# Operations of a fused attention and mixture-of-experts kernel moved within the engines' orders: bias columns, norm seeds, tanh, parts of the first units, mask rows

## The reference, cut to what matters

```
x = x + xattn(ctx, layernorm(x), mask, mask, W_src, b_src, W_tgt, b_tgt, W_out, b_out)   # x: 8 x 512 x 256
x = x + ffn(layernorm(x), gate_w, w_gate, w_up, w_down, sw_gate, sw_up, sw_down)

xattn: k, v = split((ctx @ W_src.T + b_src) * mask);  q = (x @ W_tgt.T + b_tgt) * mask    # 8 heads of 32
       scores = where(mask == 0, -inf, q k / sqrt(32));  update = softmax(scores) v
       out = concat([x, update]) @ W_out.T + b_out
ffn:   scores = sigmoid(l2norm(x) @ l2norm(gate_w).T);  the 8 largest of 16, divided by their sum = combine
       out = sum over 16 experts of combine_e * (silu(x Wg_e) * (x Wu_e)) Wd_e  +  a shared expert without combine
```

## Time and profile before

| | us |
|---|---|
| median of 3 runs (lowest, highest) | 1065.43 (1065.13, 1066.44) |
| profiled execution, span from its first to its last instruction | 1056.2 |
| what lies around the span (median less span) | 9.2 |
| PE busy, share of the span | 1012.5, 96% |
| DVE, ACT, POOL busy | 647.5, 465.9, 389.0 |
| mean granted clock of PE, of full speed | 0.992 |

### The profile page before, as it was taken

One profiled execution on the slowest core, in us unless ns is written; L12 is line 12 of the kernel. 1 busy time (PEld: TensorE's weight loads), 2 busy tenths in 40 slices (PEclk: granted clock), 3 DMA queues, 4 the chain that ended last, 5 costly groups with the idle time before them and its releaser, 6 DMA issues.

```text
span 1056.2 us, 14941 instructions
## 1 busy us (share of the span) xinstructions
PE 1012.5 (96%) x5198; PEld 773.3 (73%) x5198; DVE 647.5 (61%) x1469; ACT 465.9 (44%) x865; POOL 389.0 (37%) x355
## 2 busy tenths in 40 slices
PE   4789999999999998899999999999999999999998
PEld 3656767676767665567888888888888888888886
DVE  5877777877777557355565555555555555555544
ACT  3346565656665646545323323333333333332322
POOL 3379797879797967345210010010010100100000
PEclk9899999999999999999999999999999999999999
DMA  7343433434333223324222121121220230221220
GB/s 239 104 131 78 131 81 111 108 84 131 73 110 75 65 65 105 92 86 131 75 80 61 52 80 50 61 81 40 72 80 31 71 90 20 91 80 31 93 68 20
DMA packets 65674, 87.87 MB, mean 83 GB/s; under 512 B 10720, under 2 KB 31088, under 8 KB 65600
## 3 DMA queue, kind: packets, MB, share of 16 engines
q1 hardware_dynamic: 63680, 84.83, 28.0%
q10 hardware_dynamic: 1920, 2.10, 0.6%
HBM read 56.97 MB, written 4.46 MB: 58 GB/s over the span
## 4 chain that ended last, share of the span: by engine, by line
PE 91%; DVE 4%; ACT 2%; SPq 1%; issue 1%; DMA 1%; POOL 0%; DVEq 0%; ACTq 0%
PE ps L653 50%; PE pst L653 18%; PE ps L732 6%; PE ps L759 5%; PE pst L748 5%; PE ps L659 4%; PE ps L772 1%; DVE mx L1201 1%; ACT e_buf L868 1%; SPq L606 1%; PE ps L811 1%; SPq L541 1%; ACT ctx_h L868 0%; DVE wsrc_l L1148 0%; PE ps L812 0%
## 5 line engine op out<-in xcount | busy, mean ns | idle before, releaser
L653 PE MATMUL ps<-x_h,weights 128*128 128x512 f32 x1088 | 365.6, 397 | 1.4 <-DVE x L1194 0.8
L653 PEld LDWEIGHTS ps<-x_h,weights 128*128 128x128 f32 x1088 | 204.5, 188 | 51.8 <-issue 1.0
L1201 DVE TENSOR_REDUCE mx<-ps 128x1 f32<-128x512 f32 x256 | 173.3, 685 | 81.8 <-PE ps L732 80.9
L868 ACT ACTIVATE hh<-qb 128x512 fp32r<-128x512 f32 x136 | 86.0, 632 | 296.4 <-DVE qb L1315 273.7
L653 PE MATMUL ps<-x_l,weights 128*128 128x512 f32 x544 | 214.6, 395 | 0.0
L653 PE MATMUL pst<-hh,weights 128*128 128x512 f32 x544 | 194.6, 399 | 0.0
L1304 DVE TENSOR_TENSOR qb<-ps,sg 128x512 f32<-128x512 f32 x136 | 94.1, 692 | 160.2 <-PE ps L653 153.8
L868 ACT ACTIVATE e_buf<-pst 128x512 f32<-128x512 f32 x256 | 147.4, 596 | 92.8 <-PE pst L748 81.8
L1317 DVE TENSOR_TENSOR hl<-qb,hh 128x512 fp32r<-128x512 f32 x136 | 94.3, 693 | 95.0 <-ACT hh L868 95.0
L1407 POOL TENSOR_TENSOR e_sums<-e_sums,e_buf 128x1024 f32<-128x1024 f32 x60 | 143.5, 2391 | 7.2 <-ACT e_buf L868 1.2
L1359 POOL TENSOR_SCALAR ve<-mv 128x4 f32<-128x4 f32 x8 | 1.8, 226 | 347.1 <-DVE mv L1242 347.1
(11 more groups left out here) (159 smaller groups left out, 1391.5 us busy)
## 6 DMA issues: line engine op xcount, KB each, us to landing
cb<-combine_scratch SPq DMA_DIRECT2D x128, 256.0 KB, 3.2
q_stack<-q_h SPq DMA_DIRECT2D x128, 64.0 KB, 2.0
k_stack<-k_h SPq DMA_DIRECT2D x124, 64.0 KB, 2.0
ctx_raw<-in_ctxT SPq DMA_DIRECT2D x7, 1024.0 KB, 5.2
q_stack<-q_l SPq DMA_DIRECT2D x64, 64.0 KB, 2.0
out_x<-ob SPq DMA_DIRECT2D x16, 256.0 KB, 2.2
k_stack<-k_l SPq DMA_DIRECT2D x62, 64.0 KB, 2.0
x<-in_x SPq DMA_DIRECT2D x7, 512.0 KB, 6.5
```

Of the source, the lines that this page charges most:

```text
L653: ins = engine.matmul(dst, lhsT, rhs, start=start and n == 0, stop=stop and n == len(terms) - 1)
L868: return engine.activation(dst, src, func, **kw)
L1201: engine.tensor_reduce(MX[:, g % 2, h // 2, h % 2, q:q + 1], bank(step), AX.X, ALU.max).then_inc(sem("max"), 1)
```

## The change

Five edits, no arithmetic changed.

1. All eight bias rows are made at once: one more DMA loads the eight mask rows into `shift_rows` (partitions 32 to 39) in the first loads, behind the first mask, and one DVE operation of 8 x 512 in place of eight of 1 x 512 turns them. SP's waits for `mask_bias` beyond the first one go.
2. `bo` is cut into `bv` (DVE's columns), `bo` (PE) and `bo_add` (DVE); `q` of group 1 goes ahead of the first `v`, `bv` and `bo` go ahead of the first `max`.
3. In the first `ln2` chain the first ten steps come earlier, the others start later and lie closer.
4. The tanh of the gating stands at step 3, and the steps from there on are 1.8 ticks later (in the expert phase, where no ticks are, the tanh stands at step 3 as well).
5. A unit's part on ACT and DVE is cut into `silu`, `unit`, `hi_h` and `lo_h`. For the first six units they come 1.1, 1.9, 3.3 and 3.7 ticks behind PE's `gate_up`; later units keep their order.

```diff
@@ project, first, attention
-        if half == 0:
-            at(t + 2.7, ("mask_bias", c))
...
-             ("load_ctx", 1), ("k", 0, 0), ("k", 0, 1), ("mask_bias", 0), ("ws_hi", 1), ("hi_k", 0), ("ws_lo", 1), ("lo_k", 0),
+             ("load_ctx", 1), ("k", 0, 0), ("k", 0, 1), ("mask_bias",), ("ws_hi", 1), ("hi_k", 0), ("ws_lo", 1), ("lo_k", 0),
              ("bias_row", 0), ("stack", 0, 0), ("stack", 0, 1), ("stack", 0, 2), ("stack", 0, 3), ("wo",),
-             ("v", 0, 0, 0), ("q", 1), ("v", 0, 0, 1), ("out_q", 1), ("out_v", 0, 0), ("bias_row", 1)]
+             ("q", 1), ("bv",), ("v", 0, 0, 0), ("v", 0, 0, 1), ("out_q", 1), ("bo",), ("out_v", 0, 0), ("bias_row", 1)]
-    at(-13.8, ("bo",))
+    at(-13.8, ("bo_add",))
     for i, s in enumerate(chain("ln2", N_LN2, 0)):
-        at(t + 3.1 + 0.4 * i, s)
+        at(t + (2.6 + 0.3 * i if i < 10 else 8 + 0.33 * (i - 10)), s)
     for i, s in enumerate(chain("gating", N_GATE, 0)):
-        at(t + 4.3 + 0.4 * i, s)
+        at(t + 4.3 + 0.4 * i + (1.8 if i >= N_TANH else 0), s)
+    for n, when in enumerate((3.6, 7.2, 13, 16.2, 25.3, 26.6)):
+        at(t + when + 1.1, ("silu", n))
+        at(t + when + 1.9, ("unit", n))
+        at(t + when + 3.3, ("hi_h", n))
+        at(t + when + 3.7, ("lo_h", n))
@@ order
-            out.append(("gate_up", n))
+            out += [("gate_up", n), ("silu", n), ("unit", n), ("hi_h", n), ("lo_h", n)]
@@ SP and DVE
+                    engine.dma_start(f32(MR), mask).then_inc(sem("ld_rows"), 16)
-                    b = step[1]
-                    dve.wait_ge(*mask_loaded(b))
-                    if b > 1:
-                        dve.wait_ge(*row_loaded(2 * b - 3))
-                    engine.tensor_scalar(MR[:, b % 2, :], MB[96:97, b % 2, :], 0.0, MASKED, ALU.is_equal,
-                                         ALU.mult).then_inc(sem("mask_bias"), 1)
+                    dve.wait_ge(sem("ld_rows"), 16)
+                    engine.tensor_scalar(MR[:, :], f32(MR[:, :]), 0.0, MASKED, ALU.is_equal, ALU.mult).then_inc(
+                        sem("mask_bias"), 1)
@@ ACT
-                elif kind == "gating" and step[2] == 0:
+                elif kind == "gating" and step[2] == N_TANH:
```

More of the change, by code:

```diff
@@ L47 @@
 N_LN1, N_LN2, N_GROWS, N_GATE = N_SMALL1 + 4, N_SMALL2 + 4, 3 + rsqrt_steps(1) + 3, 16
+N_TANH = 3
 TODO = [(b, e) for b in range(B) for e in range(E + 1)]
@@ L400, in build @@
         BK, BT, BV = s1("bk", [128, 2]), s1("bt", [128, 2]), s1("bv", [128, 2])
-        shift_rows = s1("shift_rows", [97, 2, S], F32R)
-        MR, NM, OR = shift_rows[96:97, :, :], shift_rows[0:8, 0, 0:128], shift_rows[64:65, 0, :]
+        shift_rows = s1("shift_rows", [65, S], F32R)
+        MR, NM, OR = shift_rows[32:32 + B, :], shift_rows[0:8, 0:128], shift_rows[64:65, :]
         MX = s1("mx", [128, 2, 2, 2, 4])
@@ L583, in sync_program @@
                     sp.wait_ge(sem("q_f"), 2 * b - 2)
-                    sp.wait_ge(sem("mask_bias"), b - 1)
                     load_mask(engine, b)
@@ L591, in sync_program @@
                     g = step[1]
-                    sp.wait_ge(sem("mask_bias"), g // 2 + 1)
+                    sp.wait_ge(sem("mask_bias"), 1)
                     if g > 1:
                         sp.wait_ge(*scores_done(g - 2, 3))
-                    row = MR[:, (g // 2) % 2, :].rearrange("a (h s) -> a h s", h=1).to_broadcast([1, 4, S])
+                    row = MR[g // 2:g // 2 + 1, :].rearrange("a (h s) -> a h s", h=1).to_broadcast([1, 4, S])
                     engine.dma_start(f32(KS[g % 2][96:97, :, :]), f32(row)).then_inc(sem(f"bias_row{g % 2}"), 16)
@@ L616, in sync_program @@
                     sp.wait_ge(sem("x_bo"), B)
-                    sp.wait_ge(sem("mask_bias"), B)
                     for e in range(NR):
@@ L1035, in scalar_program @@
                     act.wait_ge(sem("ut_lo"), NG)
-                elif kind == "gate_up":
+                elif kind == "silu":
                     n = step[1]
@@ L1048, in scalar_program @@
                         copy(SG[:, n % 2, :], GP[n][0], ACT.Silu).then_inc(sem("silu"), 1)
+                elif kind == "hi_h":
+                    n = step[1]
                     b, e = TODO[n]
@@ L1177, in vector_program @@
                                                     sem("k_lo"), 1)
-                elif kind == "bo":
+                elif kind == "bv":
                     for k in range(2):
@@ L1183, in vector_program @@
                             sem("bv_cols"), 1)
+                elif kind == "bo_add":
                     dve.wait_ge(sem("bo_t"), 1)
-                    engine.tensor_tensor(BO[:, :], bank(step)[:, 0:D], BO[:, :], ALU.add).then_inc(sem("bo"), 1)
+                    engine.tensor_tensor(BO[:, :], bank(("bo",))[:, 0:D], BO[:, :], ALU.add).then_inc(sem("bo"), 1)
                 elif kind == "out_y":
@@ L1291, in vector_program @@
                     dve.wait_ge(sem("y"), COUNT["y", B - 1, 1, 1])
-                elif kind == "gate_up":
+                elif kind == "unit":
                     n = step[1]
@@ L1315, in vector_program @@
                         engine.tensor_tensor(QB[:, w, :], QB[:, w, :], CB[:, m % NC, :], ALU.mult).then_inc(sem("hc"), 1)
+                elif kind == "lo_h":
+                    n = step[1]
+                    w = n % 2
                     dve.wait_ge(sem("h_hi"), n + 1)
@@ L1422, in gpsimd_program @@
                     pool.wait_ge(sem("y_add"), COUNT["out_y", B - 1, 0, 1])
-                    pool.wait_ge(sem("mask_bias"), B)
                 elif kind in ("early_w", "split_w"):
```

## The result

| | us, median (lowest to highest, executions) |
|---|---|
| before | 1065.13 (1059.67 to 1066.44, 9) |
| changed | 1069.85 (1066.23 to 1071.05, 9) |
| ratio | 1.0054, 95% interval 1.0038 to 1.0070 |

The change makes the kernel half a per cent slower, 4.7 us. The forecast was 1066.6, "can't be told from unchanged"; its range of 1060.5 to 1070.5 holds the time, its likeliest direction is wrong.

A forecast was written before the change was run, and what follows sets the result against it. PE bounds the kernel, busy 1012.5 of 1056.2 us. 5.5 + 2.9 - 2.2 - 2.25 = 3.95 won, less 5.1 for low clock, is -1.15: span 1057.4, time 1066.6, range 1060.5 to 1070.5.

The forecast's parts named there:

- start: Kernel start up to the score behind SP's DMA chain: PE gets there earlier, 5.5 us won.
- mask rows: Seven DVE operations of 1 x 512 go, but none held PE up: 0 won.
- seeds: First norm chain: PE's wait of 2.29 and 1.7 of low clock go, 1.1 returns at xm: 2.9 us won.
- tanh: Gating: later tanh frees exponentials, but lg comes later on DVE and delays turn_c: 2.2 us lost.
- units: First units: the wait of 2.47 shrinks, but gate_up 3 and 5 wait for moved silus: 2.25 us lost.
- clock behind the new waits: PE resumes at low clock behind three new stretches of little work, 1.7 us each: 5.1 us lost.
- upper bound of 2.6: Tanh at turn_c: 2.6 us lost if sc also misses the gap between two POOL operations.
- The 421.6 of the working: Gating: earliest end of lg at 421.6 us, with the attention burst ending near 419.1, before POOL's effect.
- the low clock follows every new wait: Rival: low clock at each PE resumption, five stretches at 1.7 are 8.5 lost; 1070.0 us; chance 0.22.
- the main case: Whole kernel: new waits come, three bring low clock; 1066.6 us, own range 1063.5 to 1068.5; chance 0.42.
- the clock stays: Rival: the new waits come but PE keeps full clock, 3.95 won; say 1061.5 us; chance 0.25.

The follow-up runs named there:

- start_mask: The kernel before with edits 1 and 2 alone (bias rows at once, earlier start); 1058.18 us.
- mask_only: The kernel before with edit 1 alone (all bias rows at once); 1063.86 us.
- edits_1_2_3: The kernel before with edits 1, 2 and 3 (bias rows, start, norm's seeds); 1058.44 us.
- units_back: The changed kernel with edit 5 (units) taken back, so edits 1 to 4; 1061.96 us.
- tanh_back: The changed kernel with edit 4 (tanh) taken back, so edits 1, 2, 3 and 5; 1061.05 us.
- after_again: The changed kernel with all edits, unchanged, run once more; 1069.71 us.
- before_again: The kernel before, unchanged, profiled once more; 1063.45 us.
- lg_early: The kernel before with edits 1, 2, 3, unit 1's high and low parts late, tanh late, DVE's product with rn one maximum later, last gating steps close together; 1051.49 us.

## Why the forecast of no change was wrong

Each term, against the pair of kernels that differ in that edit:

| term | predicted | measured | from |
|---|---|---|---|
| start | 5.5 won | 5.9 won (4.0 in one pair of profiles) | start_mask, before |
| mask rows | 0 | 0 | mask_only, before |
| seeds | 2.9 won (1.7 of low clock in it) | 0.3 lost | edits_1_2_3, start_mask |
| tanh | 2.2 lost | 3.5 lost, clock included | units_back, edits_1_2_3 |
| units | 2.25 lost | 2.6 lost, clock included | tanh_back, edits_1_2_3 |
| clock behind the new waits | 5.1 lost | 5.3 lost beyond the sum of the two | after_again, the row above |

**The start** came out as forecast, counted from PE's first matmul, which in the profiles with edit 1 starts at 11.1 to 12.3 us and in the two without it at 10.8 and 11.2. Whether the extra DMA of edit 1 has a part in that is open; mask_only's median shows no loss. From that matmul the score behind SP's chain stands 5.4 us earlier in start_mask (12.25 to 59.57, for 10.84 to 63.58 in before_again). The first of its steps was smaller than I had it (`f_buf` at 24.70 for the earlier trace rows's 24.93, 1.3 earlier by that count and not 2.0). The next went as said: from the first maximum to that of the earlier trace rows's 37.25 it is 3.9 us (29.90 to 33.84) for 7.2. The stretch from `k_l` to the score is SP's, and as long as before: 19.2 us in start_mask for 19.0.

**The seeds are the step that failed.** The prediction let the wait of 2.29 go, and 1.7 of low clock with it, and gave back 1.1 for `xm`. The waits around the norm fell from 3.3 to 3.1 us: 0.15 won, not 1.2. Most of the gap is at the seed itself, where the prediction had no wait at all. DVE's seed, put where POOL works on a sum, lasted not the 0.17 of the earlier trace rows but until POOL was done, and PE stood 0.7 for a maximum behind it. The rows of DVE and POOL in the changed kernel:

```profile
385.32 1.79 DVE L1076 TENSOR_SCALAR rs_a<-ve 128x8 int32<-128x8 int32 x1
```

```profile
384.70 2.38 POOL L1414 TENSOR_TENSOR e_sums<-e_sums,e_buf 128x1024 f32<-128x1024 f32 x1
```

The waits around `xm` were forecast (1.4 and 0.8) and came as 1.2 and 1.2: ACT waits for `rn`, and three `xm` in a row hold up the next exponential. But the low clock that was booked as won with the wait of 2.29 is not won. It fell behind that wait at 388.0 to 390.2 us in three of the four profiles without edit 3; in all 13 profiles with it a stretch of 3.4 or 6.8 us begins at 395.4 to 400.7, around the waits at `xm`. In the changed kernel:

```profile
400.80:404.00 3.20, 3.20 (x14) 1.62 (x15) 1.98 (x4) 2.35 (x6) 0.58 (x1) 0.50 0.43 111
```

The seeds make up 3.2 of the 4.7 us by which the sum (1.15 lost) missed the 5.8 measured with after_again; the tanh makes up another 1.3. The 0.3 is uncertain by some 2 us, but 2.9 won would be a ratio of 0.9916, outside the interval of edits_1_2_3 (0.9931 to 0.9966).

**The tanh** had the right mechanism and too small a size. `turn_c` was released by `lg`, which ended with POOL's sum, and `sc` missed the gap between two POOL operations (1.44 for the 0.3 of the sum), as in the upper bound of 2.6. (The 421.6 of the working holds some 0.4 for the `max` matmul, which its terms, 2.1 us from 419.1 on, do not name.) The other part is clock. The prediction let the attention matmuls ahead of `turn_c` end 1.1 us earlier. They ran at low clock (2.87 us for 1.92), so that, counted from the first gating product, the `max` behind them stands only 0.1 earlier (11.95 for 12.06 in the profile before).

**The units** waited where the sum has them: 2.04 ahead of `gate_up` 3 (predicted 2.0), 3.44 ahead of `gate_up` 5 (3.0), released by silu behind `ut_h` and the table load; 0.81 ahead of `gate_up` 1 (0.7). The 0.8 that was to come back ahead of `gate_up` 6 can't be seen: from `gate_up` 5 to 6 it is 9.6 us in tanh_back for 8.8 before, with low clock in it.

**The clock.** The 5.1 and the 5.3 of the table lie close by luck, since they are not the same thing: the rows of the tanh and the units already hold the clock that each costs alone. The 5.3 is what both edits cost together beyond that (11.4 less 6.1). That it is the clock is shown as far as this. The waits are the same in the joint and in the single kernels. The mean clock is 0.987 in edits_1_2_3, 0.987 and 0.988 with one of the two edits and 0.983 with both: four thousandths lower where the single edits together would make it one higher. Five thousandths of the span are 5.3 us, an estimate. And taking the wait at `turn_c` away removes most of the stretches behind it. Why so many follow when both edits are there was not tested.

Of the prediction's rivals, "the low clock follows every new wait" is the one that the changed kernel's profile shows: low clock at the `xm` pair, behind `turn_c`, at `gate_up` 1 and 3, and twice as long at `gate_up` 5, where the main case counted three stretches. Its 1070.0 for the measured 1069.85 is partly luck, since it holds the 2.9 of the seeds as well.

**The frame.** By the profile alone before was 1058.4 us; a median of 1065.1 meant that typical executions lose more to the low clock than that profile showed (mean clock 0.992 there, 0.986 in the 29 executions). I read the distance as something outside the span. It changed no term, but the new stretches were counted against an execution that had unusually few, and the rival "the clock stays" leaned on that execution's luck at 442.55. By the mean clocks (0.983 for 0.986) a typical execution of the changed kernel loses 3.2 us more to the clock than one of the kernel before; in the sum it was 5.1 less the 1.7 of the seeds.

## What to carry to other kernels

When a step is moved out of a wait, write down the whole queue behind its new place with the time at which each neighbour's input comes: the wait mostly goes to the neighbour (seeds to `xm`, exponential to maximum), and wins only if the step finds a gap in its engine, as `lg` ahead of PE's next burst. Move the one operation that blocks (`hh` of unit 1: 4.0 us won) and not the whole class of them (units 2, 4 and 5: 6.3 us lost). Ask of every small VectorE step what GpSimd does at its new place. And compare the profiled span with the times of all executions before summing: here 2.0 to 2.3 us lay between span and time, so a median 9 us above the span meant an unusually short execution.

## What the runs showed of the hardware

- The clock behind a wait is not a property of the kernel. The two profiles of the kernel before have the same waits to 0.05 us from 380 us on, and its executions ran from 1057 to 1067 us; a wait of 2.47 was followed by full clock once, and low clock (6.8 us at 0.50) went with it another time.
- Waits of 1.17 and 1.23 us close together were followed by it too (low from 400.7 in the changed kernel).
- Some DVE operations with all operands in SBUF end with the POOL operation beside them. With two inputs, `sc` and `lg` took 1.44 and 1.96, where 0.21 was enough for `sc` between two POOL operations in lg_early; with one, the seed took 1.79 for 0.17 (`TENSOR_SCALAR` of 128x8). Others do not: in the changed kernel a reciprocal of 128x4 took 0.17 at 419.75 in the middle of POOL's sum (418.82 to 421.20). Maxima that read PSUM keep their 0.69. The Trainium skill ("SBUF — State Buffer", "Who interferes with whom") says that two inputs in SBUF contend with a GpSimd operation that reads SBUF, and that a tensor_scalar can in some modes; the trace agrees.
